# First expert stage of a graph network with experts: mixing weights repeated by a transfer and turned half way through the first up product, down products in four banks, routing in one piece

## What is computed

```
def _routing_weights(xf, Wr, br, Wgate, bgate):      # -> (N, 16)
    gp = softmax(xf @ Wr + br)                        # 4 sets: best two kept, cut at 0.9, renormalised
    ...
    ep = softmax(einsum('nd,gde->nge', xf, Wgate) + bgate)   # 4 experts of each set: the same
    ...
    return (w_group[:, :, None] * w_exp * SCALE).reshape(N, E)     # SCALE 0.5

tw = _routing_weights(xf, Wr, br, Wgate, bgate)
for e in range(16):
    h = silu(xf @ W1[e]) * (xf @ W3[e])
    out = out + tw[:, e:e + 1] * (h @ W2[e])
```

## Time and profile before

| | |
|---|---|
| median of 3 runs | 2429.84 us (2429.34 to 2432.61) |
| profiled execution, its own time | 2421.65 us |
| its span | 2419.9 us |
| mean granted PE clock | 0.969 of full speed |
| busy over the span | PE 2269.3 us (94%), DVE 1794.4 us (74%), ACT 1150.4 us (48%), POOL 675.4 us (28%) |
| the stage of the change | from 399 to 1168 us |

### The profile page before, as it was taken

One profiled execution on the slowest core, in us unless ns is written; L12 is line 12 of the kernel. 1 busy time (PEld: TensorE's weight loads), 2 busy tenths in 40 slices (PEclk: granted clock), 3 DMA queues, 4 the chain that ended last, 5 costly groups with the idle time before them and its releaser, 6 DMA issues. The chain is left out here.

```text
span 2419.9 us, 33046 instructions
## 1 busy us (share of the span) xinstructions
PE 2269.3 (94%) x10550; PEld 1815.3 (75%) x10550; DVE 1794.4 (74%) x4258; ACT 1150.4 (48%) x2136; POOL 675.4 (28%) x624
## 2 busy tenths in 40 slices
PE   6799986899999999999789999999997899999998
PEld 4577665688888888888668888888876677777776
DVE  8588796888888888886556755555566688888886
ACT  7565322445445454454442222222235767667652
POOL 6455022222122221210222221222233334333320
PEclk9899987999999999999899999999998899999999
DMA  5211133132231322311443344333356566666631
GB/s 166 60 54 53 19 127 104 60 98 89 69 105 60 99 88 70 105 53 49 158 161 126 125 146 134 129 129 133 130 160 202 112 181 153 148 175 159 152 109 48
DMA packets 155872, 271.87 MB, mean 112 GB/s; under 512 B 35538, under 2 KB 36178, under 8 KB 155478
## 3 DMA queue, kind: packets, MB, share of 16 engines
q1 hardware_dynamic: 123014, 203.00, 25.0%
q0 software_dynamic: 32720, 67.19, 12.8%
HBM read 185.82 MB, written 100.41 MB: 118 GB/s over the span
## 5 line engine op out<-in xcount | busy, mean ns | idle before, releaser
L2415 ACT ACTIVATE conv_h<-conv_h 128x512 f32<-128x512 f32 x79 | 50.0, 632 | 306.1 <-DVE conv_h L2344 306.1
L2892 POOL DMA_INDIRECT next_own<-message,net_slot_d x75 | 125.4, 1672 | 149.7 <-DMA next_own<-own 132.3
L2313 DVE TENSOR_TENSOR conv_yl<-conv_pty,conv_yh 128x512 fp32r<-128x512 f32 x79 | 54.6, 691 | 149.0 <-ACT conv_yh L2405 141.0
L68 PE MATMUL conv_p<-conv_w_hi,conv_yh 128*128 128x512 f32 x316 | 132.4, 419 | 1.6 <-DVE conv_yl L2313 1.6
L68 PE MATMUL d_po<-shared_wq_hi,d_hh 128*128 128x512 f32 x316 | 129.5, 410 | 2.6 <-DVE rows_rows L1523 0.2
L1373 POOL TENSOR_TENSOR d_rs<-d_ve,net_half_neg 128x4 f32<-128x4 f32 x37 | 37.3, 1007 | 337.0 <-DVE d_ve L1431 283.8
L68 PE MATMUL d_pc<-d_xh,shared_wv_hi 128*128 128x512 f32 (+1 forms) x320 | 128.6, 402 | 0.0
L68 PE MATMUL d_pa<-d_xh,xp_w_hi 128*128 128x512 f32 (+1 forms) x320 | 128.1, 400 | 0.0
L70 PE MATMUL conv_p<-conv_w_hi,conv_yl 128*128 128x512 f32 x316 | 126.5, 400 | 0.0
L69 PE MATMUL conv_p<-conv_w_lo,conv_yh 128*128 128x512 f32 x316 | 126.2, 399 | 0.0
L70 PE MATMUL conv_p<-conv_w_hi,conv_hl 128*128 128x512 f32 x316 | 125.6, 397 | 0.0
(11 more groups left out here) (621 smaller groups left out, 7173.4 us busy)
## 6 DMA issues: line engine op xcount, KB each, us to landing
conv_yin<-y SPq DMA_DIRECT2D x79, 256.0 KB, 2.7
h<-conv_h SPq DMA_DIRECT2D x79, 256.0 KB, 2.0
own<-xp_own_buf SPq DMA_DIRECT2D x79, 256.0 KB, 2.0
next_own<-own SPq DMA_DIRECT2D x79, 256.0 KB, 4.5
next_x<-y SPq DMA_DIRECT2D x79, 256.0 KB, 2.9
out<-d_res SPq DMA_DIRECT2D x79, 256.0 KB, 2.6
y<-d_y SPq DMA_DIRECT2D x78, 256.0 KB, 2.2
d_x<-in_x SPq DMA_DIRECT2D x10, 1024.0 KB, 7.4
```

Of the source, the lines that this page charges most:

```text
L68: te.matmul(out, lhs[0], rhs[0], start=first, stop=False, skip_group_check=True)
L2313: v.tensor_tensor(lo[:, t % 2, :], bank[t % 2][:], hi[:, t % 2, :].bitcast(F32), ALU.subtract)\
L2415: act_.activation(h[:, t, :], h[:, t, :], ACT.Relu).then_inc(h_made, 1)
L2892: pool.indirect_dma_start(own[n][:, t, :], None, k.message2[:, :], bass.IndirectOffsetOnAxis(ap=k.slot["d"][:, T * g + t:T * g + t + 1], a ...
```

## The change

It has four parts, in the first expert stage alone.

1. The mixing weights stay float32 and are turned by one transpose instead of two, in the middle of the first up product of the group (`half_way`) instead of behind it. The two steps that made `parts` go, so the routing has 24 steps. A group's bank `pmix`, the matmul `spread` and its constants go.
2. ACT copies the turned weights in four pieces of 16 partitions by 128 into `mix_rows` (16 x 512), ahead of `tanh` of chunk 0 instead of behind it. SP then issues a transfer inside SBUF that writes each of the 16 rows to 8 partitions (`widen_mix`, 256 KB), and DVE multiplies with this copy (`scale_mix`). For chunk 0 the multiplication stands behind `low(g + 1, n1, 0)`.
3. The four down products of a group get four banks: `po[0]`, `po[1]`, `pc[1]`, `pa[1]`. The waits of tiles 2 and 3 go, and the up product of chunk 1 now waits until all four `back` of the group before are done. The other up products wait for the gate product of the chunk two before, and no longer for the mixed one.
4. The routing is one piece: only `front1` and `front1_end` stand between its steps, and all four `back` follow it.

```diff
-        expert = c.sb("expert", [P, P])
-        expert2 = c.sb("expert2", [P, P])
-        expert_r = c.sb("expert_r", [P, P], F32R)
...
-        mix = c.sb("mix", [P, T, EXPERTS0])
-        parts = c.sb("parts", [P, T, HALF_P], F32R)
-        mix_t = c.sb("mix_t", [P, GR], F32R)
+        mix = c.sb("mix", [P, T, QUAD])
+        mix_rows = c.sb("mix_rows", [EXPERTS0, GR])
+        mix_wide = c.sb("mix_wide", [P, GR])
...
+        down_bank = [po[0], po[1], pc[1], pa[1]]
...
+            def widen_mix(g):
+
+                sp.wait_ge(hidden, KC * g + 2)
+                sp.wait_ge(mix_out, T * g + T)
+                rows = mix_rows[:, cols(g)]
+                sp.dma_start(mix_wide[:, cols(g)], rows.unsqueeze(1).broadcast_to([EXPERTS0, PER, rows.shape[1]]))                  .then_inc(mix_in, 16)
+
             def body(i, c_):
 
+                if c_ and in_range(i, c_, 0):
+                    widen_mix(i * XS + c_)
...
+            def scale_mix(g, cc):
+                h = act_out[:, cc % 2, cols(g)]
                 v.wait_ge(gated, 8 * g + 2 * cc + 2)
-                v.wait_ge(mixed, g + 1)
-                v.tensor_tensor(h, h, pmix[:, cols(g)], ALU.mult).then_inc(hidden, 1)
+                v.wait_ge(mix_in, 16 * g + 16)
+                v.tensor_tensor(h, h, mix_wide[:, cols(g)], ALU.mult).then_inc(hidden, 1)
...
                 chunk(g, 0)
                 if mid:
                     low(g + 1, n1, 0)
+                scale_mix(g, 0)
                 low_hidden(g, 0)
...
                 if mid:
-                    def first_back():
-                        back(g, u, 0)
-                        if front:
-                            front1(i, c_ + 2)
-
-                    between = {7: first_back, 9: lambda: back(g, u, 1)}
-                    if front:
-                        between[15] = lambda: front1_end(g + 2)
-                    routing(g + 1, between)
-                    back(g, u, 2)
-                    back(g, u, 3)
+                    routing(g + 1, {7: lambda: front1(i, c_ + 2), 15: lambda: front1_end(g + 2)} if front else {})
+                    for t in range(T):
+                        back(g, u, t)
...
             def mix_copy(g):
                 act_.wait_ge(mix_turned, g + 2)
-                for b in range(2):
-                    act_.activation(tile_pairs(mix_t, b)[pair_rows[b]], ptr[pair_rows[b], 0:2 * P].rearrange("p (a n) -> p a n", a=2),
-                                    ACT.Copy).then_inc(mix_out, 1)
+                if g:
+                    act_.wait_ge(hidden, KC * g + 2)
+                for t in range(T):
+                    act_.activation(mix_rows[:, t * P:t * P + P], ptr[t * QUAD:t * QUAD + EXPERTS0, 0:P], ACT.Copy, scale=0.25)\
+                        .then_inc(mix_out, 1)
...
+                mix_copy(g)
                 tanh(g, 0)
-                mix_copy(g)
...
-            def up(g, n, cc, name, out, done):
-                if name == "w1":
-                    pe.wait_ge(hidden, 4 * g + cc + 1)
+            def up(g, n, cc, name, out, done, half_way=None):
+                if name == "w1" and g + cc > 1:
+                    pe.wait_ge(gated, 8 * g + 2 * cc - 2)
+                if name == "w1" and cc == 1 and g:
+                    pe.wait_ge(x2_made, 4 * g + 2)
                 sl = slice(cc * P, cc * P + P)
                 for kc in range(KC):
+                    if half_way and kc == KC // 2:
+                        half_way()
...
-            def spread(g):
-                pe.wait_ge(hidden, KC * g + 2)
-                pe.matmul(pmix[:, cols(g)], expert_r[:], mix_t[:, cols(g)], start=True, stop=True).then_inc(mixed, 1)
-
             def turn_mix(g):
                 pe.wait_ge(route, NROUTE * g + NROUTE)
-                for a_ in range(2):
-                    last = pe.transpose(ptr[:, a_ * P:a_ * P + P],
-                                        parts[:, 2 * a_:2 * a_ + 2, :].rearrange("p t n -> p (t n)").bitcast(F32), k.ident[:])
-                last.then_inc(mix_turned, 1)
+                pe.transpose(ptr[:, 0:P], mix[:].rearrange("p t n -> p (t n)"), k.ident[:]).then_inc(mix_turned, 1)
...
-                    if cc == 0:
-                        pe.wait_ge(x2_made, 4 * g + t + 1)
+                    if cc == 0 and g and t < 2:
+                        pe.wait_ge(x2_made, 4 * g - 4 + t + 1 + 2)
                     pe.wait_ge(hl_made, 4 * g + cc + 1 + 2)
-                    last = split3(pe, po[t % 2][:], (hh[:, cc, sl], hl[:, cc, sl]),
+                    last = split3(pe, down_bank[t][:], (hh[:, cc, sl], hl[:, cc, sl]),
```

54 lines of the change are left out of this document (18 added, 36 removed).

## The result

| | before | after |
|---|---|---|
| median of four runs, us | 2430.35 (2429.34 to 2432.61) | 2415.15 (2413.54 to 2419.49) |
| ratio, 95% interval | | 0.9942 [0.9929, 0.9956] |
| profiled execution, us: time / span | 2421.65 / 2419.9 | 2415.40 / 2413.5 |
| changed stage, first norm to last `finish` on ACT, us | 768.81 | 756.35 |
| mean period of groups 1 to 18, us | 37.82 | 36.94 |

The kernel is 0.58% faster, 15.2 us by the medians. Forecast: 2417.6 us, 2.5 us above what was measured. The interval of the ratio stands for a gain of 10.7 to 17.3 us. The spans of the two profiled executions differ by only 6.4 us, but the stage, read by itself, by 12.46 (forecast 12.2).

The account below looks back on a forecast made before the run. PE was taken to bound the steady groups. Less PE work (-17.5 us), the late mixing load (+4.8) and the stage's ends (+0.5) sum to -12.2 us: 2417.6 us from a median of 2429.84, range 2410 to 2428.

Parts of the forecast that it names:

- the cliff of the transfer: DVE's first multiplication: past 4.7 + 0.14 us from issue to landing, each further 1 us costs 18 us.
- the ends of the stage: Group 0 and the last, short group: gain of 0.4 to loss of 1, and loss of 0 to 1.5; together 0.5 us lost.
- The stall of the down products: PE's down products, waiting for `back`: four banks remove both waits, gaining 0.58 us in each of 19 groups.
- `spread` and one transpose: PE, each group: one matmul (0.23 us) and one transpose of two (0.11 us) go.
- DVE's lag: DVE at the fourth gate product: it comes 0.24 us late, and its routing as well.
- The wait of the mixing load: PE's load of the mixing transpose waits 0.39 us for the routing, costing 0.27 a group, 4.8 us over 18 groups.
- My first rival: Mixing transpose on PE: no new wait, DVE's lag disappears in an uncounted gap; -17 us, 2413; chance 15%.
- my likeliest case: Whole kernel: the summed forecast with a stall of 0.1 to 0.45 us at the mixing transpose; 2413 to 2423 us; 61%.
- The transfer: SP's copy inside SBUF: lands 2.2 to 4 us after issue, within 4.7 us of cover, costing nothing in steady groups.
- Second `low` and third turn: DVE's second `low` moves to T + 5.30, PE's third turn to T + 6.42; 0.14 us left, no stall.
- the slower one: DVE's first multiplication: transfer lands late, PE stalls at its third turn; slower by 0.2% from a 5.8 us landing; 11%.
- The rival that the wait takes the gain: Mixing transpose on PE: routing lags over 0.7 us, PE loses 0.65 to 1.2 us; 2425 to 2434 us; 13%.

Follow-up runs that it names:

- the probe: Changed kernel plus five lone 256 KB transfers at the stage's end, from differing source partitions: 4.4, 3.5, 3.1, 2.3 us, and 3.0 from every eighth partition.
- the third kernel: Changed kernel with two down-product banks and `back` inside the routing again, keeping transfer and half-way turn: 2439.29 us, beside 2426.68 for the kernel before.

## Why the prediction was right

The gain of the banks, the smaller work on PE and the cliff of the transfer came out as forecast. Two terms did not, the price of the late mixing load and the ends of the stage. Their misses point opposite ways and nearly cancel, so that the closeness of the total is in part luck. By its own steps:

- **The stall of the down products**: right. Forecast 0.58 us a group, measured 0.59 with the banks alone. The 25 steps take 5.67 us (5.7 said), and no load waits for `back`.
- **`spread` and one transpose**, 0.34 us: right. From 37.23 (banks alone) these 0.34 lead to 36.89, and the steady groups of the changed kernel take 36.90.
- **DVE's lag**: the mechanism was right, its size wrong. The fourth gate product no longer waits for PE: it starts at 683.04, right behind the row before it. But the lag with which the routing follows is not 0.24. From the routing's first step at 685.78 to the next group's first up matmul at 693.91 are 8.13 us. Without a lag it would be 8.18 (727.19 - 718.43 - 0.58), with mine 7.94, and with the banks alone it is 8.16. So DVE lags by 0.03 to 0.05 us. I carried 0.56 to 0.6 us to the fourth gate product. The second and third stand only 0.35 later after T (T + 9.10 and T + 14.45, before T + 8.75 and T + 14.10, means of 16 groups), and 0.35 + 0.23 - 0.55 = 0.03.
- **The wait of the mixing load**: there as said, but smaller, and at no price. Forecast were a wait of 0.39 and a cost of 0.27 us a group, 4.8 in all. Measured is a wait of 0.28 (0.2 to 0.3 in most groups), and 37.23 - 0.34 leaves 0.01 us for its cost. Two terms were mis-sized. One is the lag above. The other is the grace of a load: I took 0.12 us from the down products (a wait of 0.42 for a cost of 0.29), and here it is 0.25 to 0.3, as one and three more steps show. The rows hint at why. In the kernel before, the first matmul behind the longer wait of the down products (0.55 us) starts 0.28 late, and its follower another 0.11. Behind a transpose those 0.11 are lost with and without a wait, so that a wait doesn't add them. No run tested this. My first rival ("no new wait at all", since the lag disappears; 2413 us) describes the steady groups better than my likeliest case: the lag did all but disappear, and the period is 36.90 against its 36.90 and my 37.15.
- **The transfer**: lands after 4.4 us. I took 2.2 to 4, so it lies beyond what I took. Here the Trainium skill (SBUF — State Buffer, Door 1: The DMA port swizzle) gave the better estimate, 4.5 us, and the probe agrees with its rule on source partitions at the ends: 4.4 us from the first 16, 2.3 us from all 128. Between them the fit is looser: the first 32 and the first 64 partitions reach the same 8 ports by that section of the Trainium skill, and here they took 3.5 and 3.1 us. My argument "same size and same queue as the store" was the wrong likeness: the store reads all 128 partitions. The cover was smaller as well, 4.5 us and not 4.7: the issue is at T - 2.6, not T - 2.8, since ACT's norm ends only at 658.78 and its copies take 1.15 us and not 1.05.
- **Second `low` and third turn**: right. The second `low` is at T + 5.16 (said 5.30, before 4.70), and the turn doesn't wait. Its slack is about 0.4 us, not 0.14; part of that is the 0.14 by which the second `low` is earlier than said.
- **The ends of the stage**: wrong. Over the 17 periods from group 1 to group 18 the change brings 15.1 us, where my step gives 17 x 0.65 = 11.1. The rest of the stage becomes 2.6 us longer, where my terms make it 1.1 shorter: a miss of 3.7 us. The two misses cancel, which is why the total (12.46 against 12.2) looks better than its parts. For group 0 I gave a loss of 1 for a landing of 4 us. There the transfer took 4.8 us, and the third turn is 2.5 us late, since ACT's copy stands behind the norm of the next group at 432.27 and the `low` stands behind the multiplication. Reordering this group alone gave 2.2 us back, reordering the last one 1.3.
- **The rivals**: the slower one didn't happen, but it was near. Beyond 0.4 us of further delay each us costs a us a group, and more where the clock falls; a turn 1.37 us later, or a second transfer, makes the kernel slower than before. By the measured slack the loss begins at a landing of 4.4 + 0.4 = 4.8 us (4.84 said), and the net gain of 0.69 us a group (12.46/18) is used up at 5.5, as I said; the smaller cover and the larger slack cancel. The figure "at 6.5 it would be 2436" is a slip: by its own terms, 18 x (6.5 - 4.84) - 12.2 above 2429.84, it is 2447. The rival that the wait takes the gain is shown in the third kernel, where the routing is late: the banks are what keeps it away.

## What to carry to other kernels

Price the parts of a change one by one, and in both orders: here one part alone gave the whole measurable gain, and the other alone was a loss. An operation that is issued far ahead is free only as long as its cover; write down cover and landing, and the distance between them (here none at the instruction that asks, and 0.4 us on the way to the engine that sets the pace), since the next change to any neighbour can use it up. And look at the first and the last pass of a loop apart: an order that is right for the steady groups may stand badly there, and a branch for these two groups gave back 3.2 to 3.6 us.
